# Graph attention with residual layer norm on one core: inverse sums spread from repeated columns, divides between turns, and some transfers issued by ScalarE

## The chip, the cores and the metric

The kernel runs on one core of one Trainium2 chip. The metric is the time of one execution on the device in microseconds (us). The core's engines run side by side and are called TensorE (PE: matmuls, with its weight loads as PEld), VectorE (DVE), ScalarE (ACT), GpSimd (POOL) and SyncE (SP, which here only issues transfers). Sixteen DMA engines move the data.

## What is computed

```python
x (8, 1024, 384) f32, adj (8, 1024, 1024) bool, four 384x384 weights, four biases
q, k, v = heads(x @ Wq + bq), heads(x @ Wk + bk), heads(x @ Wv + bv)      # 6 heads of 64
scores = einsum('bhqd,bhkd->bhqk', q, k) / sqrt(64)
probs = softmax(scores + where(adj, 0.0, -9e15), axis=-1)
ctx = einsum('bhqk,bhkd->bhqd', probs, v)
out = layernorm(x + ctx @ Wf + bf)                                        # eps 1e-5, no affine part
```

## The kernel before

Each of the 8 batches is a list of 24 slots. A slot handles one pair of heads and one tile of 128 queries: TensorE makes the scores of both heads against 1024 keys (`scores`), VectorE adds the mask and takes the row minimum (`mask_scores`, line 676, once per head), ScalarE takes the exponential and the row sum (`exponential`, line 606), and VectorE turns every 32x32 block of the result in place (`turn_squares`, line 683, once per head). Two slots are a group: 256 queries of one pair of heads, 12 groups to a batch. I write g5 for group 5; its second slot is slot 11.

When a group's four turns are done, SyncE issues 16 transfers, `move_square` at line 307, each of which takes 32 partitions of `prob` to 32 partitions of `prob_t` (128 KB). That finishes the transpose of the probabilities. `move(b, group, 0)` issues the first eight and `move(b, group, 1)` the last eight; between the two stand, in some slots, a load of the next batch's x (`load_x`, line 358, slots 4, 6, 11 and 12 by `X_LOADS`), a store of finished rows (line 370) or a load of residual rows (line 364). SyncE works through all this in order. `prob` and `prob_t` have two buffers each, so the masks of group g wait until the transfers of g - 2 have landed.

Two and a half to three slots later TensorE multiplies `prob_t` with v (`mix`, line 515, 16 matmuls in full f32). The rows of the softmax are not divided before that. VectorE takes the reciprocals of the row sums (`invert_sums`, line 688), GpSimd writes them on the diagonals of four 128x128 blocks (`make_diagonal`, line 803), and TensorE multiplies a block of ones with these (`spread_inverses`, line 437), which gives the inverse sums of the queries along the free axis in all 64 partitions of a head. ScalarE copies them to `context` (line 581), and `divide` (line 693) multiplies them with the mix. ScalarE and GpSimd then split the context into a high and a low part (lines 613 and 809) for the output projection.

What else TensorE does stands in the table `STEADY`: per slot a list of jobs, run behind the slot's scores in the order written. ("i", g, ..) is the spread of inverse sums of g, ("m", g, ..) its mix, ("p", n, ..) the output projection of tile n, ("q"/"k"/"v", ..) projections, ("x", ..) transposes of the next batch's x. All jobs but m rotate over three PSUM banks. The other engines follow the same table. In a slot with an m job the order on VectorE is: two masks, two turns, divide. The layer norm's inverse root is 12 tiny steps of Newton's method on GpSimd (`find_root`); the last group of rows of the last batch is scaled on VectorE when they are done.

Of the kernel before, what the change touches and what calls it, by code (L numbers as in the profile page):

```python
# [6 lines left out]
F32 = mybir.dt.float32  # L7
# [3 lines left out]
ALU = mybir.AluOpType  # L11
# [54 lines left out]
X_LOADS = {4: (0, 0), 6: (0, 1), 11: (1, 0), 12: (1, 1)}  # L66
# [51 lines left out]
def graph_attention(nc, x, adj, wq, bq, wk, bk, wv, bv, wf, bf, out):  # L118
# [15 lines left out]
    with ExitStack() as ctx:  # L134
# [22 lines left out]
        diag = sb("diag", [P, 4, P], F32)  # L157
# [4 lines left out]
        ones = sb("ones", [P, HS], F32)  # L162
# [31 lines left out]
        ones_done = sem("ones_done")  # L194
# [11 lines left out]
        diag_done = sem("diag_done")  # L206
# [103 lines left out]

        block = ctx.enter_context(nc.Block())
# [4 lines left out]
        def _(sp):  # L316
# [26 lines left out]
            def move(b, group, part):  # L343
                if part == 0:
                    sp.wait_ge(squared, at(b, UNITS, 4 * group + 4))
                    sp.wait_ge(mixed, at(b, GROUPS, group + 1))
                for ahead in (2 * part, 2 * part + 1):
                    for a in range(4):
                        move_square(sp, group, a, (a + ahead) % 4)

            def load_x(b, half, i):
                last_x = ("x", FT - 1, 1 - half, 1)
                if half == 0 and b.mode == "first":
                    sp.wait_ge(job_done, 3)
                else:
                    sp.wait_ge(job_done, done_through(b, last_x, 1 - half))
                row = S + (4 * half + 2 * i) * P
                sp.dma_start(x_in[:, 2 * i:2 * i + 2, :], x_rows[bass.ds(at(b, S, row), GQ), :].rearrange(
                    "(t p) h -> p t h", p=P)).then_inc(x_loaded[i], 16)
# [13 lines left out]
            def body(b):  # L373
                for s in range(SLOTS):
                    if s % 2 == 1:
                        move(b, s // 2, 0)
                    if s in X_LOADS and b.mode != "last":
                        load_x(b, *X_LOADS[s])
# [4 lines left out]
                    if s % 2 == 1:  # L383
                        move(b, s // 2, 1)
# [15 lines left out]
        def _(pe):  # L400
# [489 lines left out]
```

## Time and profile before

| | us |
|---|---|
| median of 3 runs | 1284.17 (1280.67 to 1289.34) |
| the profiled execution's own time | 1280.71 |
| its span, first to last instruction | 1278.9 |
| TensorE busy | 1177.3 (92%) |
| VectorE busy | 1057.7 (83%) |
| ScalarE busy | 737.2 (58%) |
| GpSimd busy | 655.1 (51%) |
| DMA engines busy, mean | 78.9% on the queue SyncE issues to, 250.13 MB |

The page of the profile gives busy times by engine, a picture of the span in 40 slices, the chain of work that ended last, and groups of instructions by line. Questions to the trace give waits, the chain or the timeline of a stretch in order of time, and busy times of a stretch. An engine's busy share says little here by itself: which wait ends last in a stretch decides.

### The profile page before, as it was taken

The page shows a single profiled execution, that of the slowest core. Times are in us where ns is not written, and L with a number is a line of the kernel's source. Part 1 is how long each engine was busy: PE and PEld are TensorE (multiplying, and loading weights), DVE is VectorE, ACT ScalarE, POOL GpSimd, SP SyncE. Part 2 cuts the span into 40 slices and gives each one's busy share as a digit, 9 for nine tenths or more (in the row PEclk, how much of TensorE's full clock was granted, in tenths as well). Part 3 has the DMA queues.
Part 4 walks back from the last instruction along what each step waited for, and adds up shares of the span by engine and source line. Part 5 has one row for each costly group of instructions (what it writes and reads, how often), then busy time and mean ns, then how long its engine had stood idle before and what let it go on. Part 6 is the DMA issues. An engine that isn't in the chain of part 4 may idle for free.

```text
span 1278.9 us, 23768 instructions
## 1 busy us (share of the span) xinstructions
PE 1177.3 (92%) x8406; PEld 867.3 (68%) x8406; DVE 1057.7 (83%) x1619; ACT 737.2 (58%) x1404; POOL 655.1 (51%) x956
## 2 busy tenths in 40 slices
PE   6998999999999899989999899998999999998874
PEld 5866777666776677666776667766677666776642
DVE  5788887988789887889869889698887988789882
ACT  4665665656556575566655565555664656555540
POOL 1335662646536565474545665355762656535533
PEclk9999999999999999999999999999999999999997
DMA  5678877897778877888877978779877897868883
GB/s 163 148 192 234 190 198 192 201 237 175 201 191 215 228 189 195 198 222 201 205 186 188 237 186 211 181 188 248 190 195 186 205 242 176 206 165 204 211 195 96
DMA packets 111607, 251.66 MB, mean 197 GB/s; under 512 B 27904, under 2 KB 62336, under 8 KB 111488
## 3 DMA queue, kind: packets, MB, share of 16 engines
q1 hardware_dynamic: 111488, 250.13, 78.9%
q8 instruction: 67, 1.10, 0.4%
q14 instruction: 52, 0.43, 0.1%
HBM read 36.11 MB, written 12.58 MB: 38 GB/s over the span
## 4 chain that ended last, share of the span: by engine, by line
PE 53%; SPq 16%; DVE 16%; ACT 5%; issue 4%; DMA 3%; POOL 2%; DVEq 0%; POOLq 0%
PE context_ps L515 17%; SPq L307 15%; PE score_ps L500 13%; PE job_ps L406 7%; DVE prob L683 7%; PE job_ps L408 6%; PE job_ps L407 6%; ACT prob L606 5%; DVE prob L676 5%; DMA prob_t<-prob 3%; PE job_ps L437 2%; DVE res L700 1%; DVE stats L707 1%; POOL xt_lo L793 1%; SPq L370 1%
## 5 line engine op out<-in xcount | busy, mean ns | idle before, releaser
L606 ACT ACTIVATE prob<-prob,row_min 128x1024 f32<-128x1024 f32 x384 | 440.9, 1149 | 252.8 <-DVE row_min L676 252.8
L676 DVE CUSTOM_DVE_ANT_0 prob<-score_ps,mask 128x1024 f32<-128x1024 f32 x384 | 454.7, 1221 | 144.8 <-PE score_ps L500 122.7
L683 DVE STREAM_TRANSPOSE prob<-prob 128x1024 f32<-128x1024 f32 x384 | 458.9, 1233 | 31.7 <-ACT prob L606 31.7
L515 PE MATMUL context_ps<-prob_t,v_all 128*64 128x256 f32 x3072 | 359.8, 388 | 40.0 <-DMA prob_t<-prob 39.8
L515 PEld LDWEIGHTS context_ps<-prob_t,v_all 128*64 128x64 f32 x3072 | 236.0, 140 | 151.3 <-issue 58.6
L775 POOL TENSOR_SCALAR mask<-adj_in 128x1024 f32<-128x1024 uint8 x64 | 68.1, 1064 | 169.6 <-DVE row_min L676 156.2
L500 PE MATMUL score_ps<-k_hi,q_hi 64*128 64x512 f32 x768 | 140.7, 444 | 10.5 <-DVE row_min L676 9.7
L809 POOL TENSOR_TENSOR context_lo<-context,context_hi 128x256 fp32r<-128x256 f32 x96 | 70.6, 735 | 142.0 <-ACT context_hi L613 142.0
L406 PE MATMUL job_ps<-xt_hi,weight_hi 128*128 128x256 f32 (+1 forms) x423 | 142.5, 337 | 0.6
L797 POOL TENSOR_TENSOR q_lo<-raw,q_hi 128x256 fp32r<-128x256 f32 x95 | 69.5, 734 | 139.1 <-ACT raw L598 139.1
L407 PE MATMUL job_ps<-xt_lo,weight_hi 128*128 128x256 f32 (+1 forms) x423 | 135.5, 320 | 0.0
L408 PE MATMUL job_ps<-xt_hi,weight_lo 128*128 128x256 f32 (+1 forms) x423 | 135.5, 320 | 0.0
L500 PE MATMUL score_ps<-k_lo,q_hi 64*128 64x512 f32 x768 | 120.6, 391 | 0.0
L500 PE MATMUL score_ps<-k_hi,q_lo 64*128 64x512 f32 x768 | 119.9, 389 | 0.0
L613 ACT ACTIVATE context_hi<-context 128x256 fp32r<-128x256 f32 x96 | 40.0, 417 | 114.5 <-DVE context L693 114.4
L803 POOL TENSOR_TENSOR diag<-ident,inv_sum 128x512 f32<-128x512 f32 x96 | 100.0, 1042 | 8.6 <-PE job_ps L437 4.3
L301 POOL TENSOR_SCALAR res<-res,mean_var,inv_dev 128x384 f32<-128x384 f32 x62 | 101.9, 1650 | 0.0
L406 PEld LDWEIGHTS job_ps<-xt_hi,weight_hi 128*128 128x128 f32 x423 | 79.5, 188 | 32.3 <-issue 25.9
L500 PEld LDWEIGHTS score_ps<-k_hi,q_hi 64*128 64x128 f32 x768 | 57.2, 184 | 64.1 <-issue 39.0
L797 POOL TENSOR_TENSOR k_lo<-raw,k_hi 128x512 fp32r<-128x512 f32 x46 | 58.8, 1288 | 74.5 <-ACT raw L598 74.4
L581 ACT ACTIVATE context<-job_ps 128x256 f32<-128x256 f32 x96 | 37.0, 386 | 95.4 <-PE job_ps L437 75.4
L408 PEld LDWEIGHTS job_ps<-xt_hi,weight_lo 128*128 128x128 f32 x423 | 79.6, 188 | 6.6
(73 smaller groups left out, 1693.1 us busy)
## 6 DMA issues: line engine op xcount, KB each, us to landing
prob_t<-prob SPq DMA_DIRECT2D x1536, 128.0 KB, 2.4
res<-in_x_dram SPq DMA_DIRECT2D x32, 384.0 KB, 4.0
out_dram<-res SPq DMA_DIRECT2D x32, 384.0 KB, 3.0
x_in<-in_x_dram SPq DMA_DIRECT2D x30, 384.0 KB, 4.1
adj_in<-in_adj_dram SPq DMA_DIRECT2D x31, 256.0 KB, 2.9
res<-in_x_dram SPq DMA_DIRECT2D x1, 768.0 KB, 7.0
prob_t<-in_L_gnn_Wk_dram SPq DMA_DIRECT2D x1, 576.0 KB, 4.3
prob_t<-in_L_gnn_Wq_dram SPq DMA_DIRECT2D x1, 576.0 KB, 8.4
```

The source lines that it names most:

```text
L301: engine.tensor_scalar(res[:, n, :], res[:, n, :], mean_var[:, group % 2, tile, 0:1], inv_dev[:, group % 2, tile:tile + 1], ALU.subtract, ...
L307: queue.dma_start(prob_t[32 * c:32 * c + 32, group % 2, a].rearrange("p q h n -> p (q h n)"), prob[32 * a:32 * a + 32, group % 2, c].rearr ...
L406: pe.matmul(dst, left_hi, right_hi, start=(t == 0), stop=False)
L407: pe.matmul(dst, left_hi, right_lo, start=False, stop=False)
L408: last = pe.matmul(dst, left_lo, right_hi, start=False, stop=(t == FT - 1))
L500: last[head] = pe.matmul(score_ps[:, head, keys], q_part[rows, pair, q], k_part[rows, pair, keys], start=(n == 0), stop=(n == 2))
L515: last = pe.matmul(context_ps[64 * head:64 * head + 64, 0:GQ], v_all[:, kt, col:col + HS], keys, start=(kt == 0), stop=(kt == TT - 1))
L606: nc.scalar.activation(probabilities(t), probabilities(t), ACT.Exp, scale=-1.0, bias=row_min[:, ring:ring + 1], accum_out=row_sum[:, s // ...
L676: nc.vector.tensor_tensor_reduce(probabilities(t), in_quarters(score_ps[:, head, :]), in_quarters(mask[:, s % 2, :]), 1.0, HUGE, ALU.add, ...
L683: nc.vector.transpose(probabilities(t), probabilities(t)).then_inc(squared, 1)
L797: nc.gpsimd.tensor_tensor(lo, copy[:, 0:width], hi, ALU.subtract).then_inc(lo_done, 1)
L803: nc.gpsimd.tensor_tensor(diag[:], ident[:].unsqueeze(1).to_broadcast([P, 4, P]), inv_sum[:, group % 2, :].unsqueeze(2).to_broadcast([P, 4 ...
```

## The change

1. `spread_inverses` no longer multiplies ones with a diagonal. For each head and each tile of 128 queries it takes one column of `inv_sum`, repeated 64 times by a stride of zero, as the weights, and the identity as the moving operand: four matmuls of 128 columns where there were two of 256. `make_diagonal`, its tile and its semaphore are gone; TensorE waits for the reciprocals themselves.
2. On VectorE the divides of a slot stand between its two turns.
3. The loads of x's second half (slots 11 and 12 on SyncE) are issued by ScalarE, both behind its eviction of the job ("x", 2, 0, 1) in slot 11.
4. The last eight squares of the last group of the last batch are issued by ScalarE in place of SyncE.
5. The last Newton iteration of the program runs on VectorE. In slot 9 the output projection stands behind the transpose of x.

```diff
-    9: [("q", 0, 2, 0), ("p", 0, 0, 0), ("x", 0, 0, 1)],
+    9: [("q", 0, 2, 0), ("x", 0, 0, 1), ("p", 0, 0, 0)],
-X_LOADS = {4: (0, 0), 6: (0, 1), 11: (1, 0), 12: (1, 1)}
+X_LOADS = {4: (0, 0), 6: (0, 1)}
...
             def spread_inverses(b, job):
-                pe.wait_ge(diag_done, at(b, GROUPS, job[1] + 3))
-                for head in range(2):
-                    last = pe.matmul(job_bank(b.mode, job)[64 * head:64 * head + 64, 0:GQ], ones[:],
-                                     diag[:, 2 * head:2 * head + 2, :], start=True, stop=True)
+                group = job[1]
+                pe.wait_ge(inverted, at(b, GROUPS, group + 1))
+                for qt in range(2):
+                    for head in range(2):
+                        col = 2 * head + qt
+                        last = pe.matmul(job_bank(b.mode, job)[64 * head:64 * head + 64, qt * P:(qt + 1) * P],
+                                         inv_sum[:, group % 2, col:col + 1].to_broadcast([P, HS]), ident[:],
+                                         start=True, stop=True)
                 last.then_inc(job_done, 1)
...
+                    if s == SLOTS:
+                        move(nc.scalar, b, GROUPS - 1, 1)
...
                             evict(b, job)
+                            if job == ("x", FT - 1, 0, 1):
+                                for i in range(2):
+                                    load_x(nc.scalar, b, 1, i)
...
                         turn_squares(b, 2 * s)
-                        turn_squares(b, 2 * s + 1)
                     for job in work:
                         if job[0] == "m":
                             divide(b, job[1])
+                    if s < SLOTS:
+                        turn_squares(b, 2 * s + 1)
...
                     if s == SLOTS + 1:
-                        dve.wait_ge(root_ops, at(b, 4 * ROOT_OPS, 4 * ROOT_OPS))
+                        dve.wait_ge(root_ops, at(b, 4 * ROOT_OPS, 3 * ROOT_OPS))
+                        find_root(nc.vector, b, 3)
                         scale_rows(nc.vector, 3)
```

In a batch in the middle, these are SyncE's issues of slots 9 to 13 before (line 370 stores rows, 307 moves squares, 364 loads residual rows, 358 loads x):

```order
L370 DMA out_dram<-res 128x2x384
L307 DMA prob_t<-prob 32x1024 x8
L364 DMA res<-in_x_dram 128x2x384
L307 DMA prob_t<-prob 32x1024 x8
L358 DMA x_in<-in_x_dram 128x2x384
L307 DMA prob_t<-prob 32x1024 x8
L358 DMA x_in<-in_x_dram 128x2x384
L307 DMA prob_t<-prob 32x1024 x8
L370 DMA out_dram<-res 128x2x384
```

and these now (383, 303 and 377 are the same issues in the changed file):

```order
L383 DMA out_dram<-res 128x2x384
L303 DMA prob_t<-prob 32x1024 x8
L377 DMA res<-in_x_dram 128x2x384
L303 DMA prob_t<-prob 32x1024 x24
L383 DMA out_dram<-res 128x2x384
```

The two loads of x have left the queue: one stood between the two halves of g5's squares, one ahead of g6's. On ScalarE they stand here now, in slot 11 behind the copies of x and ahead of the next slot's copy of inverse sums and exponentials:

```order
L603 ACTIVATE xt_hi<-job_ps 128x2x8x32
L612 ACTIVATE raw<-job_ps 128x512
L314 DMA x_in<-in_x_dram 128x2x384 x2
L597 ACTIVATE context<-job_ps 128x256
L622 ACTIVATE prob,row_sum<-prob,row_min 128x4x256 x2
```

So whatever ScalarE pays for issuing them lies ahead of slot 12's copy and exponentials.

VectorE in a slot with a mix, before:

```order
L676 ISA prob,row_min<-score_ps,mask 128x4x256
L676 ISA row_min 128x1
L683 STREAM_TRANSPOSE prob<-prob 128x4x256 x2
L693 TENSOR_TENSOR context<-context_ps,context 128x256
L676 ISA prob,row_min<-score_ps,mask 128x4x256
```

and now (697, 704 and 715 are these lines in the changed file):

```order
L697 ISA row_min 128x1
L704 STREAM_TRANSPOSE prob<-prob 128x4x256
L715 TENSOR_TENSOR context<-context_ps,context 128x256
L704 STREAM_TRANSPOSE prob<-prob 128x4x256
L697 ISA prob,row_min<-score_ps,mask 128x4x256
```

The divide, with its wait for the mix, now has a turn behind it instead of the next slot's mask.

## Rows read from the trace of the kernel before

**Rows 1.** The page: busy us of each engine, share of span, instructions.
```profile
PE 1177.3 (92%) x8406; PEld 867.3 (68%) x8406; DVE 1057.7 (83%) x1619; ACT 737.2 (58%) x1404; POOL 655.1 (51%) x956
```
**Rows 2.** The page: the chain that ended last, by engine and by line.
```profile
PE 53%; SPq 16%; DVE 16%; ACT 5%; issue 4%; DMA 3%; POOL 2%; DVEq 0%; POOLq 0%
PE context_ps L515 17%; SPq L307 15%; PE score_ps L500 13%; PE job_ps L406 7%; DVE prob L683 7%; PE job_ps L408 6%; PE job_ps L407 6%; ACT prob L606 5%; DVE prob L676 5%; DMA prob_t<-prob 3%; PE job_ps L437 2%; DVE res L700 1%; DVE stats L707 1%; POOL xt_lo L793 1%; SPq L370 1%
```
**Rows 3.** Waits, whole span: who waited for whom, us in total, times, longest.
```profile
PE context_ps L515 <- DMA prob_t<-prob: 39.8, 26, 3.6
...
DVE prob L676 <- DMA prob_t<-prob: 20.5, 16, 3.0
...
PE job_ps L406 <- POOL context_lo L809: 12.5, 9, 1.9
...
PE job_ps L437 <- POOL diag L803: 4.5, 1, 4.5
```
**Rows 4.** Timeline of TensorE, slot 10 of batch 4: start us, us, what.
```profile
701.14 0.65 PE L437 MATMUL job_ps<-diag,ones 128*64 128x256 f32 x4
...
701.72 0.66 PE L416 MATMUL job_ps<-ident,x_in 128*128 128x128 f32 x4
...
702.31 3.67 PE L515 MATMUL context_ps<-prob_t,v_all 128*64 128x256 f32 x32
```
**Rows 5.** Timeline of SyncE's queue, slots 11 and 12 of batch 4.
```profile
712.82 4.96 SPq L307 DMA_DIRECT2D prob_t<-prob  x8
717.83 0.59 SPq L358 DMA_DIRECT2D x_in<-in_x_dram  x1
718.46 5.08 SPq L307 DMA_DIRECT2D prob_t<-prob  x8
723.58 0.58 SPq L358 DMA_DIRECT2D x_in<-in_x_dram  x1
```
**Rows 6.** Chain of batch 4 in order of time, start us, us, what.
```profile
722.94 3.37 DMA prob_t<-prob
...
726.45 5.36 PE context_ps L515 x32
...
786.48 2.28 DMA prob_t<-prob
```
**Rows 7.** Stretches: busy us by engine, granted clock, DMA share, GB/s.
```profile
719.80:721.20 1.40, 1.40 (x14) 1.40 (x13) 1.40 (x3) 0.67 (x2) 1.01 (x3) 1.00 0.95 343
...
721.60:724.40 2.80, 2.25 (x16) 1.27 (x16) 2.63 (x4) 2.80 (x8) 2.80 (x3) 1.00 1.04 250
1250.00:1255.00 5.00, 0.48 (x4) 0.32 (x4) 0.45 (x2) 0.42 (x1) 3.91 (x14) 0.75 0.91 207
```
**Rows 8.** Timeline of ScalarE, end of slot 11 and slot 12 of batch 4.
```profile
712.36 0.60 ACT L596 ACTIVATE raw<-job_ps 128x512 f32<-128x512 f32 x1
713.79 0.38 ACT L581 ACTIVATE context<-job_ps 128x256 f32<-128x256 f32 x1 [0.83 <-PE job_ps L437]
715.79 1.15 ACT L606 ACTIVATE prob<-prob,row_min 128x1024 f32<-128x1024 f32 x1 [1.61 <-DVE row_min L676]
```
**Rows 9.** Chain of the program's end in order of time.
```profile
1247.39 0.51 SPq L307
...
1256.81 2.44 DMA prob_t<-prob
...
1271.37 0.18 DVE var_eps L714
1271.57 0.18 DVE inv_dev L717
...
1275.11 0.48 DVE res L301
```
**Rows 10.** Timeline of VectorE, slot 12 of the last batch.
```profile
1175.92 1.23 DVE L676 CUSTOM_DVE_ANT_0 prob<-score_ps,mask 128x1024 f32<-128x1024 f32 x1 [0.27 <-DMA prob_t<-prob]
...
1181.23 1.23 DVE L676 CUSTOM_DVE_ANT_0 prob<-score_ps,mask 128x1024 f32<-128x1024 f32 x1
```

More of the change, by code:

```diff
@@ L309, in move_square, with load_x, find_root, result @@
                             ).then_inc(landed[group % 2], 16)
+        def load_x(queue, b, half, i):
+            last_x = ("x", FT - 1, 1 - half, 1)
+            if half == 0 and b.mode == "first":
+                queue.wait_ge(job_done, 3)
+            else:
+                queue.wait_ge(job_done, done_through(b, last_x, 1 - half))
+            row = S + (4 * half + 2 * i) * P
+            queue.dma_start(x_in[:, 2 * i:2 * i + 2, :], x_rows[bass.ds(at(b, S, row), GQ), :].rearrange(
+                "(t p) h -> p t h", p=P)).then_inc(x_loaded[i], 16)
+        def find_root(engine, b, group):
+            engine.wait_ge(guess_done, at(b, 4, group + 1))
+            guess, var = inv_dev[:, group % 2], var_eps[:, group % 2]
+            ops = 0
+            def result(instruction):
+                nonlocal ops
+                ops += 1
+                instruction.then_inc(root_ops, 1)
+                engine.wait_ge(root_ops, at(b, 4 * ROOT_OPS, group * ROOT_OPS + ops))
+            for _ in range(NEWTON_STEPS):
+                result(engine.tensor_tensor(newton[:], guess, guess, ALU.mult))
+                result(engine.tensor_tensor(newton[:], newton[:], var, ALU.mult))
+                result(engine.tensor_scalar(newton[:], newton[:], -0.5, 1.5, ALU.mult, ALU.add))
+                result(engine.tensor_tensor(guess, guess, newton[:], ALU.mult))
+        def move(queue, b, group, part):
+            queue.wait_ge(squared, at(b, UNITS, 4 * group + 4))
+            queue.wait_ge(mixed, at(b, GROUPS, group + 1))
+            for ahead in (2 * part, 2 * part + 1):
+                for a in range(4):
+                    move_square(queue, group, a, (a + ahead) % 4)
         block = ctx.enter_context(nc.Block())
@@ L341, in load_adjacency @@
                     "(q p) k -> p q k", p=P)).then_inc(adj_loaded, 16)
[L343 to L359, printed above, removed]
             def load_residual(b, group):
@@ L382, in body @@
                         load_residual(b, RES_LOADS[s])
-                    if s % 2 == 1:
-                        move(b, s // 2, 1)
+                    if s % 2 == 1 and (s < SLOTS - 1 or b.mode != "last"):
+                        move(sp, b, s // 2, 1)
                     if s % 6 == 1 and (s // 6 < 3 or b.mode != "last"):
@@ L840, in body @@
                         next_mask(b, s // 6 + 1, s % 6 - 4)
-                    if s == 2 and b.mode == "first":
-                        make_diagonal(b, 0)
-                    for job in work:
-                        if job[0] == "m" and job[1] + 1 < GROUPS:
-                            make_diagonal(b, job[1] + 1)
                     for group in contexts_split(b.mode, s):
```

39 lines of the change are left out of this document (5 added, 34 removed).

## The prediction

> **What bounds the kernel now.** I read the page first. TensorE is busy 92% of the span and VectorE 83% [rows 1], but the chain that ended last is TensorE for only 53%; SyncE's queue holds 16% and VectorE 16% [rows 2]. So the bound changes inside a batch. The chain in order of time shows where: from the end of a batch to about slot 6 it is an unbroken row of matmuls, and from slot 7 on it passes VectorE, SyncE's issues, a landing and the mix. The waits say the same in sum: TensorE waits 39.8 us for landed squares in 26 places and VectorE another 20.5 us in 16 [rows 3]. Out of 1279 us that is not much, so a change that removes no TensorE work can give only a few per cent at most. The queue's timeline shows the tightest place, slots 11 and 12: eight squares, a load of x, eight squares, a load of x, without a pause [rows 5]. The last square of g5 is issued at 722.94, takes 3.37 us to land, and the mix waits for it until 726.45; a square with no load around it lands in 2.28 us [rows 6].
>
> **The change part by part.** All sums are against the profiled execution's own 1280.71 us; the median of the runs, 1284.17, is 3.5 us above it, and I shift by that at the end.
>
> *The spread.* Before, one spread holds TensorE from 701.14 to 701.72, 0.58 us, for four records of 256 columns (each f32 matmul leaves two) [rows 4]. They run in two pairs, one for each 64-wide half of the array. Now there are eight records of 128 columns, four pairs. No row has 64-wide weights with 128 columns. The nearest is the transpose of x: four records of 128 columns, each with its own 128x128 f32 weights, hold TensorE from 701.72 to 702.31, 0.59 us [rows 4]. So a new weight load per 128 columns does not lengthen the record, and four pairs should take what four such records take. The mix behind it (32 records, 64-wide weights, in 3.67 us) shows that pairs do overlap. I take +0.02 us a spread. If pairs did not overlap, eight records would cost twice the 0.59, so the other bound is +0.6 us; below, zero, since the columns streamed are the same. There are 96 spreads, and the chain has 2% of the span in L437 [rows 2], 25.6 us, or 44 spreads at 0.58. The rest lie ahead of a mix that waits for its landing anyway. Sum: 44 x 0.02 = +1 us (0 to +26).
>
> *The diagonal gone.* GpSimd loses 96 operations, but TensorE waited for one only once, 4.5 us [rows 3], ahead of the last mix, which waits longer for its landing. The context's low part no longer stands behind a diagonal, and the divide comes a turn earlier, so TensorE's wait for it, 12.5 us in 9 places [rows 3], should vanish, helped by x standing ahead of the projection in slot 9. I count almost nothing: where I looked at it, in slot 9, the chain runs through VectorE's turns, which have no gap there. That cover gone, it would be worth 1.3 us a batch. I take -0.5 us for all of it.
>
> *The divide between the turns.* VectorE does the same work. The price comes where the mix is not done when the first turn ends, since the second turn then waits too, and the next mask behind it. In slot 12 of the last batch mask and mix start together at 1175.9, released by the same landing. The mix needs 3.67 us [rows 4]; the next mask ran at 1181.23, behind both turns and the divide [rows 10]. With the new order the divide starts at 1179.6, when the mix ends, and the turn ends about 1.6 us later, at 1181.2. The next mask is where it was, within 0.1 us, and it needs the scores, which TensorE only starts behind the mix. So the cost is zero as long as the divide waits for nothing else; uncovered it would be 0.1 us in the 11 even slots of 8 batches, +9 us. I take 0.
>
> *The loads of x.* Per batch but the last, SyncE's queue loses two issues of 0.59 and 0.58 us [rows 5]. The first stands inside g5's chain, so its last square is issued 0.63 us earlier. It also has company in landing now (3.37 against 2.28 us), and that need not get better: both loads are issued by ScalarE from 712.96 on, where the copy of x ends, all inside g5's transfers. ScalarE can afford it: it has 0.83 us of idle time before the next copy, which would slip by about 0.4 us, and 1.61 us before the next exponential [rows 8]. The DMA engines are what is short. With squares alone and a backlog they moved 250 GB/s at a share of 1.04, against 207 GB/s at 0.91 when one queue feeds them at its own pace [rows 7]. In the microsecond and a half in which mostly a load ran, the rate was 343 GB/s [rows 7]. Work from 712.8 on: 16 squares, 2.1 MB at 250 GB/s, 8.4 us; two loads and the residual rows issued just before, 1.18 MB at 343 GB/s, 3.4 us; with about a microsecond for the first packet and the landing that ends at 725.6, where it was 726.3. Where the queue was late for g6 as well, more is won. I take -0.9 us a batch: 7 x 0.9 = -6.3 us. Bounds: the second load's 0.39 MB at the squares' 250 GB/s, 1.6 us, less the issue of 0.63, is a loss of 1.0 us each, +7 us; and the issue with all of the late landing, 0.6 + 1.1 us, plus the 0.6 us where g6 finds the queue still busy, is -2.3 us each, -16 us.
>
> *The last squares.* The chain has 16 issues from 1247.39 on, the last at 1256.81, and the landing at 1259.25 [rows 9]. Split over two queues, if only issuing counts, the last is issued 8 x 0.63 = 5.0 us earlier. If the DMA engines count, 2.10 MB at 250 GB/s take 8.4 us from about 1248.1 and land at 1256.9: -2.3 us. At 207 GB/s nothing is won. I take -2.3 (0 to -5.0), for both halves read the same 32 partitions of `prob` in the same order.
>
> The Trainium skill has a rule here, in "SBUF — State Buffer", Door 1: The DMA port swizzle: 32 neighbouring partitions reach only 8 of 16 DMA ports, about 218 GB/s at most. By it, since both queues would start from the same 32 partitions, the 2.10 MB would take 9.6 us and the saving would be 1.1 us. The 207 GB/s agree with it, the 250 GB/s do not, so it holds at most for squares that share their partitions.
>
> *Newton on VectorE.* Its last tiny step starts at 1271.57, 0.20 us behind the one before it, and the scaling at 1275.11, 3.54 us later, with 12 steps of GpSimd between [rows 9]. Thirteen steps of 0.20 are 2.6 us: -0.9 us (0 to -1).
>
> Sum: +1 - 0.5 + 0 - 6.3 - 2.3 - 0.9 = **-9.0 us**, to 1271.7 in the profile and **1275 us** in the median, 0.7% less.
>
> **The rivals.** *The queue's relief pays in full (0.22).* TensorE's clock speaks for it. Before g5's mix it idled and then ran the mix in 5.36 us instead of 3.67 [rows 4, 6]. If the earlier landing saves that too, each batch gives up to -2.3, and the end 5.0: 1 - 0.5 - 16 - 5.0 - 0.9 = -21, 1263 us. Against it: the DMA engines are already saturated in this stretch [rows 7].
>
> *The transfers only trade places (0.20).* The engines, not the queues, set g5's landing and the end's. Then the loads give 0 and the end, by the port rule or by 207 GB/s, 1 us or none: 1 - 0.5 - 1 - 0.9, about -1, 1283 us. For it speaks the share of 1.04 [rows 7].
>
> *The short matmuls don't overlap (0.10).* It is the one that ends slower: 44 spreads at +0.6 are +26 us, less the other gains of 10, +16: 1300 us. It decides against the change from +0.23 us a spread on. Against it stands the transpose's 0.59 us for as many weight loads at twice the width [rows 4].
>
> **How the numbers follow.** The forecast has 0.48, and by itself 1268 to 1282. The likeliest value is 1275. The range takes in most of the first rival and all of the second, and cuts off the last: 1263 to 1289. This kernel's runs spread over 0.7%, so about 1% is what a measurement can tell from no change; that is below 1271.3 or above 1297. Faster: the first rival and the forecast's lower edge, 0.29. Slower: the last rival where nothing else pays, 0.08. Same: 0.63.
>
> **What would show it.** The mix should start 0.6 us behind a spread, as now; 1.0 or more means that pairs don't overlap. g5's last landing should come 12.6 us behind its first issue instead of 13.5, and ScalarE's two issues should cost it no idle exponential. The last group's squares should land 9.5 us after their first issue, not 11.9. TensorE's wait for the context's low part should be near nothing, and the scaling should start 2.6 us behind the guess. It would be wrong if VectorE's new wait for the mix grew to over 0.3 us a slot, or if SyncE's issues took longer than 0.59 us while ScalarE issues too.

## The result, and the profile after

| | before | after |
|---|---|---|
| median, us | 1286.29 (4 runs) | 1306.65 (1296.31 to 1312.39, 4 runs) |
| ratio | | 1.0149 [1.0109, 1.0189] |
| profiled execution, us | 1280.71 | 1307.82 |
| its span, us | 1278.9 | 1305.9 |
| mean granted clock of TensorE | 0.986 | 0.972 |

The change makes the kernel 1.5% slower. I had forecast 1275 us, 0.7% less, and the time lies outside the range.

The page of after, busy time by engine and the chain that ended last, beside [rows 1, 2]:

```profile
PE 1191.2 (91%) x8790; PEld 889.9 (68%) x8790; DVE 1062.6 (81%) x1631; ACT 735.6 (56%) x1404; POOL 555.6 (43%) x847
...
PE 53%; SPq 14%; DVE 13%; DMA 5%; ACT 5%; issue 5%; POOL 3%; ACTq 1%; POOLq 0%; DVEq 0%
```

TensorE is busy 14 us more with the same arithmetic, GpSimd 100 us less without the diagonals, and the chain now has 5% in landings where it had 3%. The waits of after, beside [rows 3] (who waited for whom, us in total, times, longest):

```profile
PE context_ps L532 <- DMA prob_t<-prob: 69.1, 26, 8.0
...
DVE context L715 <- PE context_ps L532: 43.9, 43, 13.8
...
DVE prob L697 <- DMA prob_t<-prob: 36.0, 21, 5.1
```

TensorE waits for landed squares in 26 places as before, but 69.1 us where it was 39.8; VectorE's masks wait 36.0 instead of 20.5, and the divide now waits for the mix.

Where in a batch? I worked out from both traces, as means over batches 1 to 6, when each group's squares landed and what the mixes did:

| mean over batches 1 to 6, us | before | after |
|---|---|---|
| length of a batch | 153.7 | 158.2 |
| g4: last issue's end to last landing | 1.71 | 5.00 |
| g5: the same | 2.55 | 3.78 |
| g6: the same | 1.94 | 1.71 |
| idle of TensorE before the mixes of g4, g5, g6 | 0.59, 2.49, 0.13 | 4.01, 0.14, 2.80 |
| first start to last start in those mixes | 3.29, 4.39, 3.27 | 5.06, 3.25, 4.84 |

(A mix at full clock measures 3.24 to 3.30 here; the timeline adds the last record's own length.) Batch 0 is 148.1 and 148.3 us, and the last batch 182.4 in both, to the end of the program. So the whole loss of the profiled execution, 27 us of span, is 6 x 4.4 us in the middle batches. (By the medians the change costs 20 us: the profiled execution of before is the fastest of its four.) It lies in three slots: g4's squares, which had landed in time, are late, and the mixes of g4 and g6 run long.

Batch 4 shows why. SyncE's queue in after, beside [rows 5] (start us, us, what):

```profile
725.13 4.96 SPq L303 DMA_DIRECT2D prob_t<-prob  x8
730.13 0.58 SPq L377 DMA_DIRECT2D res<-in_x_dram  x1
730.81 20.34 SPq L303 DMA_DIRECT2D prob_t<-prob  x24
```

The first line is the last eight squares of g4, issued until 730.09; then the residual rows, then g5's sixteen squares and eight of g6, without the loads of x between. ScalarE in after, beside [rows 8]:

```profile
728.22 1.15 ACT L622 ACTIVATE prob<-prob,row_min 128x1024 f32<-128x1024 f32 x1
729.07 0.41 ACTq L314 DMA_DIRECT2D x_in<-in_x_dram  x1
...
729.51 0.76 ACTq L314 DMA_DIRECT2D x_in<-in_x_dram  x1
...
730.56 0.60 ACT L612 ACTIVATE raw<-job_ps 128x512 f32<-128x512 f32 x1
732.00 0.38 ACT L597 ACTIVATE context<-job_ps 128x256 f32<-128x256 f32 x1 [0.84 <-PE job_ps L453]
```

The loads stand in the program behind the copy of x, L612. They leave at 729.07 and 729.51, the first while ScalarE is still in an exponential, and the copy ends only at 731.16. The queue of ScalarE hands over the first DMA while five operations that stand ahead of it, the copy the last, have yet to start; nothing made it wait. So the loads go out 2.1 us before the copy's end, the first 1.02 us before g4's last issue ends. The chain of the stretch, beside [rows 6], shows what that does:

```profile
729.50 4.60 DMA prob_t<-prob
734.10 0.14 issue
734.23 0.93 PE context_ps L532 x5
```

The last square of g4 takes 4.60 us to land, where a square with no load around it took 2.28 and g5's last one, with a load in its own queue, 3.37 [rows 6]. The packets show who is served in the meantime. From 730.75 to 732.00 (queue: packets, MB, share of the 16 engines):

```profile
q10 hardware_dynamic: 151, 0.23, 75.5%
q1 hardware_dynamic: 15, 0.00, 0.7%
```

q10 is ScalarE's queue, q1 SyncE's. g4's last square has been issued and has not landed, and for 1.25 us all the bytes that move are those of the loads. TensorE's timeline of the same batch:

```profile
731.29 0.66 PE L453 MATMUL job_ps<-ident,inv_sum 128*64 128x128 f32 x8 [0.68 <-DVE res L722]
734.23 5.36 PE L532 MATMUL context_ps<-prob_t,v_all 128*64 128x256 f32 x32 [2.28 <-DMA prob_t<-prob]
...
745.25 0.66 PE L453 MATMUL job_ps<-ident,inv_sum 128*64 128x128 f32 x8
...
760.26 6.26 PE L532 MATMUL context_ps<-prob_t,v_all 128*64 128x256 f32 x32 [4.26 <-DMA prob_t<-prob]
```

and stretches of it (us, busy us by engine with counts, then the granted clock, DMA share, GB/s):

```profile
734.30:736.00 1.70, 1.70 (x12) 1.26 (x14) 1.70 (x3) 0.52 (x1) 1.21 (x7) 0.66 1.12 346
736.00:739.50 3.50, 3.50 (x24) 2.32 (x20) 1.84 (x3) 1.87 (x4) 0.72 (x4) 0.68 1.03 247
745.80:749.40 3.60, 3.60 (x36) 2.21 (x34) 3.44 (x7) 2.84 (x6) 3.27 (x4) 1.00 0.55 121
```

Having idled for 2.28 us, TensorE runs g4's mix in 5.36 us; the granted clock is 0.66 and 0.68 of full, that is, 1.2 GHz for about two thirds of it. g5's mix, at 745.73 behind matmuls without a gap, has 1.00, 2.4 GHz, and takes 3.6 us. g6's is late again: 4.26 us idle, then 6.26 us. Before the change the same fall was paid once in four of the batches 1 to 6, at g5; after it twice in five of them, at g4 and g6.

The end of the program, SyncE's and ScalarE's queues and the chain, beside [rows 9]:

```profile
1275.76 7.26 SPq L303 DMA_DIRECT2D prob_t<-prob  x8
```

```profile
1275.76 7.93 ACTq L303 DMA_DIRECT2D prob_t<-prob  x8
```

```profile
1299.47 0.18 DVE inv_dev L739
...
1302.12 0.48 DVE res L297
```

Each queue takes over 7 us for eight issues, where one alone took 5. The last landing came at 1286.57, 10.81 us behind the first issue; it was 11.86 before. The scaling starts 2.65 us behind the guess.

### The profile page after: what moved, and what is told of

Read it like the earlier page. It is cut to its first block, busy times and chain, and to the rows that moved or that the text cites. A ratio compares the mean times of both kernels' runs of the same rounds, so it can differ in the third digit from the quotient of the medians.

```text
span 1305.9 us, 24453 instructions
## 1 busy us (share of the span) xinstructions
PE 1191.2 (91%) x8790; PEld 889.9 (68%) x8790; DVE 1062.6 (81%) x1631; ACT 735.6 (56%) x1404; POOL 555.6 (43%) x847
## 4 chain that ended last, share of the span: by engine, by line
PE 53%; SPq 14%; DVE 13%; DMA 5%; ACT 5%; issue 5%; POOL 3%; ACTq 1%; POOLq 0%; DVEq 0%
PE context_ps L532 19%; SPq L303 13%; PE score_ps L517 13%; PE job_ps L419 7%; PE job_ps L421 6%; PE job_ps L420 6%; DVE prob L704 6%; DMA prob_t<-prob 5%; ACT prob L622 5%; DVE prob L697 4%; PE job_ps L453 2%; POOL xt_lo L816 1%; SPq L383 1%; DVE res L722 1%; DVE stats L729 1%
## 5 line engine op out<-in xcount | busy, mean ns | idle before, releaser
L704 DVE STREAM_TRANSPOSE prob<-prob 128x1024 f32<-128x1024 f32 x384 | 467.0, 1236 | 31.7 <-ACT prob L622 31.7
L532 PE MATMUL context_ps<-prob_t,v_all 128*64 128x256 f32 x3072 | 375.0, 400 | 69.1 <-DMA prob_t<-prob 69.1
L532 PEld LDWEIGHTS context_ps<-prob_t,v_all 128*64 128x64 f32 x3072 | 239.3, 144 | 175.8 <-issue 88.0
L798 POOL TENSOR_SCALAR mask<-adj_in 128x1024 f32<-128x1024 uint8 x64 | 67.1, 1048 | 180.5 <-DVE row_min L697 167.3
L517 PEld LDWEIGHTS score_ps<-k_lo,q_hi 64*128 64x128 f32 x768 | 72.6, 184 | 16.7
L517 PEld LDWEIGHTS score_ps<-k_hi,q_lo 64*128 64x128 f32 x768 | 72.7, 184 | 16.4
```

The lines of the kernel that those rows point to most:

```text
L517: last[head] = pe.matmul(score_ps[:, head, keys], q_part[rows, pair, q], k_part[rows, pair, keys], start=(n == 0), stop=(n == 2))
L532: last = pe.matmul(context_ps[64 * head:64 * head + 64, 0:GQ], v_all[:, kt, col:col + HS], keys, start=(kt == 0), stop=(kt == TT - 1))
L704: nc.vector.transpose(probabilities(t), probabilities(t)).then_inc(squared, 1)
```

## The experiments

Ratios are to the kernel before, with 95% intervals. Line numbers in a diff are left out.

**Parts undone and parts alone.** First, which part costs: after without the moved loads, and before with the loads, the spread or the divide alone. e1:

```diff
-X_LOADS = {4: (0, 0), 6: (0, 1)}
+X_LOADS = {4: (0, 0), 6: (0, 1), 11: (1, 0), 12: (1, 1)}
-                            if job == ("x", FT - 1, 0, 1):
-                                for i in range(2):
-                                    load_x(nc.scalar, b, 1, i)
```

> The changed kernel with part 3 undone: SyncE issues both loads of x's second half again, in slots 11 and 12; all other parts stay. Theory Q (ScalarE's queue issues the loads ahead of its copies, while g4's last squares are still to land, and they overtake these): g4 lands 1.7 us behind its last issue again instead of 5.0, slots 11 and 12 shrink from 17.2 to about 12.2 us a batch, and the time is 1280 us or less, ratio to before 0.99 to 1.00. Rival V (the divide between the turns, or the spread, costs the time): nothing of this changes, the time stays near 1306, ratio 1.015.

Measured: 1.0002 [0.997, 1.0035], 1288.97 us. The whole loss is gone. Theory Q had hoped for more, 1280 us or less; slots 11 and 12 take 12.8 us in the trace, and g4's lag is 1.71.

e2 is before with the same lines the other way round:

```diff
-X_LOADS = {4: (0, 0), 6: (0, 1), 11: (1, 0), 12: (1, 1)}
+X_LOADS = {4: (0, 0), 6: (0, 1)}
+                            if job == ("x", FT - 1, 0, 1):
+                                for i in range(2):
+                                    load_x(nc.scalar, b, 1, i)
```

> The kernel before with part 3 alone: ScalarE issues both loads behind the job (x, 2, 0, 1) of slot 11. Theory Q: g4 lands 4 to 5 us behind its last issue, 3 to 5 us more a batch, ratio 1.015 to 1.025. Rival V: ratio 0.995 to 1.002.

Measured: 1.0095 [1.0062, 1.0129], 1303.37 us. The loads alone cost 1%, less than the 1.5 to 2.5% of theory Q and far more than rival V allows; g4's lag is 4.47 us. The profiled execution took 1289.82 us, the fastest of its ten, so what I read from the trace of e2 below is on the low side.

e3 is before with the new spread and inversion, and without diagonals:

```diff
-                    last = pe.matmul(job_bank(b.mode, job)[64 * head:64 * head + 64, 0:GQ], ones[:],
-                                     diag[:, 2 * head:2 * head + 2, :], start=True, stop=True)
+                        last = pe.matmul(job_bank(b.mode, job)[64 * head:64 * head + 64, qt * P:(qt + 1) * P],
+                                         inv_sum[:, group % 2, col:col + 1].to_broadcast([P, HS]), ident[:],
+                                         start=True, stop=True)
```

> The kernel before with part 1 alone: inverse sums spread from repeated columns, no diagonals on GpSimd. Theory Q: the spread costs TensorE 0.02 us more each, GpSimd is free 100 us more, ratio 0.998 to 1.001. Rival V: if repeated columns or the earlier waits cost anything, ratio above 1.003.

Measured: 0.9993 [0.9966, 1.002], 1286.42 us. e4 is before with the divide between the turns:

```diff
-                        turn_squares(b, 2 * s + 1)
                     for job in work:
                         if job[0] == "m":
                             divide(b, job[1])
+                    if s < SLOTS:
+                        turn_squares(b, 2 * s + 1)
```

> The kernel before with part 2 alone: the divide between a slot's two turns. Theory Q: VectorE waits for the mix in the middle of some slots, but its next mask needs scores that come behind the same mix, so ratio 0.998 to 1.002. Rival V: the wait delays turns and masks, 0.1 us or more in each of the 11 even slots with a mix and up to 1.5 us where the mix runs at 1.2 GHz, ratio 1.005 to 1.015.

Measured: 0.9999 [0.9968, 1.0029], 1288.49 us. Spread and divide, alone, are worth nothing either way, within 0.3%. Loads alone (1.0095) do not make up all of after's 1.0149, and the divide is a candidate for the rest. I took after again beside the next kernels, unchanged, and e7, which is e2 with the diff of e4:

> The changed kernel as it is, again, so that the next three stand on the same chip beside it. Ratio to before 1.012 to 1.018.

> The kernel before with parts 2 and 3, the divide between the turns and the loads on ScalarE. If the two add up to nothing more than part 3 alone, its ratio is that of the loads alone, 1.0095. If the divide's wait for a late mix makes the late landing dearer, it is 1.013 to 1.018, as the whole change.

```diff
 # e2, and:
-                        turn_squares(b, 2 * s + 1)
                     for job in work:
                         if job[0] == "m":
                             divide(b, job[1])
+                    if s < SLOTS:
+                        turn_squares(b, 2 * s + 1)
```

Measured: after again 1.0135 [1.0089, 1.0181]; e7 1.0198 [1.0164, 1.0232], 1314.55 us. So a divide that costs nothing alone doubles the price of the loads. e7 came out dearer than I had expected, and dearer than after, which has the same two parts and more; between the profiled executions 6 of the 7 us lie in batch 0, where g4's squares land 4.80 us behind their last issue in e7 and 1.87 us in after. The waits of e7:

```profile
PE context_ps L515 <- DMA prob_t<-prob: 62.3, 23, 4.8
...
DVE context L696 <- PE context_ps L515: 51.2, 47, 10.2
```

and the one of e2:

```profile
PE context_ps L515 <- DMA prob_t<-prob: 51.6, 25, 4.5
```

In these two traces TensorE waits 11 us longer for about as many landings.

**Where the loads leave, and in which queue.** Three kernels keep all of after and change only this. e5 gives both loads back to SyncE, directly ahead of g5's squares, so that they cannot pass g4's:

```diff
                 for s in range(SLOTS):
+                    if s == 11 and b.mode != "last":
+                        for i in range(2):
+                            load_x(sp, b, 1, i)
                     if s % 2 == 1:
                         move(sp, b, s // 2, 0)
```

(ScalarE's two loads behind its copy of x are taken out here, and in e6 as well.)

> The changed kernel with both loads of x issued by SyncE in slot 11, back to back, directly ahead of g5's squares: the same bytes within about 1.5 us of the time at which ScalarE issued them, but in the queue of the squares and behind g4's. If it is the second queue that lets the loads overtake g4's squares, g4 lands 1.7 to 1.9 us behind its last issue (5.0 in the changed kernel), and the ratio to before is 0.998 to 1.005, the two issues now being paid in full ahead of g5. If it is simply 0.79 MB of loads in a saturated stretch, g4 is still late by 2 us or g5 by 3 us or more, ratio 1.008 or more.

Measured: 1.0042 [1.0014, 1.0069], 1295.29 us. e6 lets ScalarE issue them behind slot 12's exponentials, where by its queue they fall among g5's squares alone, which is where my prediction had put them:

```diff
                         exponential(b, 2 * s + 1)
+                    if s == 12 and b.mode != "last":
+                        for i in range(2):
+                            load_x(nc.scalar, b, 1, i)
```

> The changed kernel with ScalarE's two loads behind the exponentials of slot 12. Their masks wait for g4's landing, so the loads can't be issued before it, and everything they meet is g5's squares, as the prediction had it. If the prediction's size for that was right, g4 lands 1.7 us behind its last issue, g5's landing gains 0.9 us a batch, and the ratio to before is 0.990 to 0.996. If loads on a second queue hold up any squares they meet, g5 lands 4 to 5 us behind its last issue instead of 2.5, ratio 1.005 or more.

Measured: 1.009 [1.0068, 1.0113], 1301.97 us. e9 leaves them in their place but makes ScalarE's queue wait until its copy of x is really done:

```diff
                             if job == ("x", FT - 1, 0, 1):
+                                act.wait_ge(job_out, out_through(b, job))
                                 for i in range(2):
                                     load_x(nc.scalar, b, 1, i)
```

> The changed kernel with a wait of ScalarE for its own copy of x ahead of the two loads, so that they are issued where the prediction had them, behind the copy, about 2 us later than in the changed kernel. If the sequencer's running ahead of its queued activations is what put the loads among g4's squares, no square of g4 is issued behind the first load now, g4 lands 1.7 to 2.5 us behind its last issue, g5 lands 3.5 to 4.7 us behind its last, and the ratio is 1.003 to 1.010, as with the loads behind slot 12's exponentials. If the place made no difference, g4 stays at 5 us and the ratio at 1.0135.

Measured: 1.0106 [1.0074, 1.0138], 1299.27 us. Means over batches 1 to 6, worked out from the traces:

| us | before | after | e5 | e6 | e9 |
|---|---|---|---|---|---|
| g4: last issue's end to landing | 1.71 | 5.00 | 1.70 | 1.70 | 1.81 |
| g5: last issue's end to landing | 2.55 | 3.78 | 2.81 | 4.70 | 4.95 |
| g5: first issue to last landing | 13.63 | 14.11 | 13.59 | 15.40 | 15.48 |

In e6 and e9 the first load leaves at most 0.33 us before g4's last issue ends, mostly after it, and g4 lands as before the change. So the overtaking made it late: its lateness goes when the loads leave later, with the same bytes in the same second queue. But the lateness then falls on g5, whose squares take 15.4 us instead of 13.6. In one queue, e5, g5's squares have nearly their old lag, but the first is issued 1.9 us behind the last turn instead of 0.7, and g5's mix is waited for 3.48 us and is slow in five of the six batches. e6's timeline of TensorE shows the two mixes side by side:

```profile
725.50 3.67 PE L532 MATMUL context_ps<-prob_t,v_all 128*64 128x256 f32 x32
...
739.43 6.58 PE L532 MATMUL context_ps<-prob_t,v_all 128*64 128x256 f32 x32 [3.30 <-DMA prob_t<-prob]
```

and its stretches, same columns as above:

```profile
725.50:729.00 3.50, 3.50 (x34) 2.60 (x32) 3.27 (x8) 1.81 (x4) 2.84 (x9) 1.00 0.95 258
739.50:743.50 4.00, 4.00 (x20) 2.54 (x22) 3.55 (x5) 2.38 (x4) 0.00 (x0) 0.50 0.95 242
```

g4's mix follows without a gap at 2.4 GHz, g5's comes behind 3.30 us of idling and starts at exactly half. The DMA engines move 242 to 258 GB/s at a share of 0.95 in both: I take them to be full, so that a load can only be fitted in by making squares wait.

**The clock as the channel.** A late landing is paid twice, as idle time and then as a slow mix. I sorted the batches 1 to 6 of ten traces (before, after, its repeat, e1 to e7) by how many mixes took over 4.2 us:

| slow mixes in the batch | batches | mean length, us | range | idle before its 12 mixes, mean us |
|---|---|---|---|---|
| 0 | 15 | 153.1 | 152.1 to 154.0 | 4.3 |
| 1 | 30 | 155.3 | 153.6 to 157.6 | 4.4 |
| 2 | 15 | 159.0 | 157.7 to 160.9 | 7.4 |

The groups hardly overlap, whatever the kernel. Over its whole trace before has 6 slow mixes, after 13, e1 4, e2 7, e7 16. Between none and one the idle time is the same, and the batch is 2.2 us longer: that is what one slow mix goes with. The second slow mix comes together with 3 us more of idling, so there the table does not say which of them costs. To part them I kept the waits and filled the idle time with matmuls nobody reads, five in e10 ahead of the mixes of g4 and g6. Their result is overwritten by the mix:

```diff
                 pe.wait_ge(context_done, at(b, GROUPS, group + 2))
+                if group in (4, 6) and b.mode != "last":
+                    for _ in range(5):
+                        pe.matmul(context_ps[:, GQ:2 * GQ], ident[:], v_all[:, 0, 0:GQ],
+                                  start=True, stop=True)
```

> The changed kernel with five idle matmuls (identity by 256 columns of v, into the unused half of the mix's PSUM bank, read by nobody) in front of the mixes of g4 and g6 in all batches but the last, where TensorE now waits 4.0 and 2.8 us for landed squares. They leave the late landing as it is and keep TensorE at work. Theory C (the late landing costs what it costs because TensorE falls to 1.2 GHz in those waits, and then runs the mix in 5.0 instead of 3.3 us with everything behind it): granted clock 0.98 or more instead of 0.97, mixes of g4 and g6 at 3.3 us, batches of 153 to 155 us instead of 158, ratio to before 0.998 to 1.005. Theory L (the lateness itself costs it): batches stay at 157 to 158 us, or grow by the idle work, ratio 1.012 to 1.02.

Measured: 1.0083 [1.0055, 1.0111], 1296.68 us, granted clock 0.986, 4 slow mixes. The ratio lies between the two theories. The mixes of g4 and g6 fall from 5.06 and 4.84 to 3.58 and 3.30 us, and a batch from 158.2 to 155.5. Batch 0, where g4 had not been late, is 151.1 us instead of 148.3 with the fill; the last batch, without a fill, is 182.4 us as in after. So of the 4.4 us a batch that the change lost in these traces, 2.7 went by the clock; by the ratios of all runs it is 0.7 of 1.5%, or nearly half. The rest stays with late landings.

e11 puts the same fill, four matmuls, in e1 ahead of g5's mix, e12 in before, and e15 is e11 again:

```diff
+                if group in (5, 99) and b.mode != "last":
+                    for _ in range(4):
+                        pe.matmul(context_ps[:, GQ:2 * GQ], ident[:], v_all[:, 0, 0:GQ],
+                                  start=True, stop=True)
```

> The changed kernel with both loads back on SyncE, as in e1_loads_back, and four idle matmuls (1.7 us) in front of the mix of g5, where it waits about 2.2 us. Theory C: no batch but the last has a mix at 1.2 GHz, all batches take 152.5 to 153.5 us, ratio to before 0.990 to 0.997. Theory L: ratio 1.000 to 1.005.

> The kernel before with four idle matmuls in front of the mix of g5 in all batches but the last, and nothing else. Theory C: the gain of e11_back_filled is the clock's, so this has it too, ratio 0.991 to 0.996, no mix of batches 0 to 6 at 1.2 GHz. If that gain needs the changed parts (spread, divide, Newton, tail), the ratio is 0.997 to 1.002.

> e11_back_filled again, on the chip of the one before: what the parts of the change other than the loads add once the clock holds. Theory C, with the prediction's sizes for them (-2.7 us): 0.2% below e12_before_filled. If the divide between the turns costs something of its own, 0 to 0.3% above it.

Measured: e11 0.9914 [0.9887, 0.994], 1276.39 us; e12 0.9917 [0.989, 0.9943], 1278.23 us; e15 0.9893 [0.9856, 0.993], 1275.25 us. The fill makes either kernel about 1% faster. e15 is 3 us below e12 in the median, as the prediction's sizes for the other parts have it (-2.7 us), but the intervals overlap. e11 in batch 4:

```profile
724.60 1.99 PE L526 MATMUL context_ps<-v_all,ident 128*128 128x256 f32 x8
...
726.97 3.67 PE L535 MATMUL context_ps<-prob_t,v_all 128*64 128x256 f32 x32 [0.38 <-DMA prob_t<-prob]
```

```profile
727.00:730.50 3.50, 3.50 (x32) 2.18 (x32) 3.27 (x5) 2.17 (x3) 0.82 (x1) 1.00 0.95 250
```

The fill ends 0.38 us before the squares have landed, and the mix has the full clock, where before the change it took 5.36 us [rows 6]. In the traces the mixes of g5 fall from a mean of 4.39 us in before to 3.30 in both e11 and e12. Yet the traces show less than the whole of the gain: the middle batches are 153.7 us in before, 153.5 in e12, 153.0 in e11 and 152.9 in e1. The reason is which execution was profiled. Those of before and e1 are each the fastest of their own runs, and e1's had the g5 mixes of batches 1 to 6 at full clock without a fill. The 93 runs of before that were taken beside the experiments have granted clocks of 0.971 to 0.987; the 15 below 0.977 took 1293.3 us on average, the 12 from 0.984 on 1283.0, and a straight line through all gives 9.3 us for 0.01. The six runs of e12 have 0.990 on average where before has 0.980: by that line, an estimate, 9 us, and 9.7 were measured between the medians. The last batch, in which nothing is filled, adds something in one kernel: it is 182.4 and 183.3 us in before and e1, 180.5 in e12, but 177.1 in e11 and 177.8 in its repeat e15, with fewer or other slow mixes. The runs may also scatter less: over ten runs each, by 8.8 us in e11 and by 13.0 in e1. So that the fill helps is measured, and that it does so by the clock agrees with the clocks of all runs; why the last batch is shorter in e11 and e15 stays open. e11 is the best kernel of this study: parts 1, 2, 4 and 5 with the fill. Its interval and e12's lie on each other, so its gain is the fill's.

One thing more can be read from these numbers, and it limits what e10 said. e10 and e11 differ only in who issues the loads and in which gaps are filled and how far, and they ran side by side: 1296.68 against 1276.39 us, 1.6%. Without fills, after and e1 are 1.5% apart. e13 below against e12 is 1.2%, without fills e2 against before 1.0%. So with fills on both sides, moving the loads costs as much as it did. Only a part of that is still the clock: it is 0.984 in e10 and 0.990 in e11 over all runs, some 6 of the 20 us by the line above. The clock explains part of what after lost against a before that itself loses it at g5; the late landings are a price of the move that these fills do not take away.

e13 and e14 use the fill of e10 to ask why the divide made the loads dearer: e13 is e2 with it, e14 is e7 with it.

```diff
+                if group in (4, 6) and b.mode != "last":
+                    for _ in range(5):
+                        pe.matmul(context_ps[:, GQ:2 * GQ], ident[:], v_all[:, 0, 0:GQ],
+                                  start=True, stop=True)
```

> The kernel before with the loads on ScalarE (as e2_loads_only, 1.0095) and five idle matmuls in front of the mixes of g4 and g6. Theory C: few slow mixes, what is left is the lateness and the idle work, ratio 1.002 to 1.007.

> The same with the divide between the turns (without the idle matmuls, e7_loads_divide, 1.0198). If the divide makes the loads dearer only through the clock, the idle matmuls take away nearly all of the difference: within 0.3% of e13_loads_filled, ratio 1.004 to 1.009. If VectorE's wait in mid-slot costs by itself, the difference of 1% stays: 1.012 to 1.018.

| | unfilled | filled |
|---|---|---|
| loads alone (e2, e13) | 1.0095 [1.0062, 1.0129] | 1.0033 [1.0008, 1.0057] |
| loads and divide (e7, e14) | 1.0198 [1.0164, 1.0232] | 1.0026 [1.0002, 1.0051] |

e14's ratio is lower still than I had expected, 1.004 at least. With the idle time filled the two can't be told apart: the medians are 1291.58 and 1293.85 us, 0.2% apart, where the ratios without fill differ by 1.0%. So the divide raises the loads' price through the clock, wholly or nearly so; the two intervals would hide a remainder of some 0.3%. How it does so I can argue but did not show: slot 10 is 5.19 instead of 5.53 us with it, the loads leave 1.7 us before g4's last issue ends instead of 1.3 on average, more squares stand behind them, and TensorE idles longer and loses the clock in 16 mixes instead of 7 (in the traces; over all runs the granted clock is 0.965 against 0.976). After's own batches fit: in batch 0 no square was issued behind the first load and g4's lag was 1.87 us, with one square it was 4.0 and 4.2, with two 4.9, with three 5.2, with four 5.7 and 6.1. The time seems to matter more than the count: in three batches of e2 no issue of a square began behind the first load, but it left 0.54 to 0.86 us before g4's last issue ended, and the lag was 3.9 to 4.1.

**The last squares.** e8 is e1 with ScalarE's eight squares started from the other half of the partitions, since the port rule that the prediction named would have made the shared partitions the limit:

```diff
             for ahead in (2 * part, 2 * part + 1):
-                for a in range(4):
+                for n in range(4):
+                    a = (n + 2) % 4 if queue is nc.scalar else n
                     move_square(queue, group, a, (a + ahead) % 4)
```

> The changed kernel with the loads back on SyncE, and of the last group's squares ScalarE's eight in another order, so that the two queues never read the same 64 partitions at a time (sources 2, 3, 0, 1 against 0, 1, 2, 3). In the changed kernel the sixteen landed 10.8 us behind the first issue, 11.9 before. If the ports of the source partitions are the limit, as the page on SBUF has it for 32 partitions, it is 8.5 us or less now; if the limit is elsewhere (issuing, or the engines' own rate of about 250 GB/s), it stays at 10 to 11 us. The time of the whole is 1.000 in ratio, within what can be measured.

Measured: 0.997 [0.9941, 1.0], 1285.03 us. The last landing is 10.91 us behind the first issue, against 10.69 in e1 and 10.81 in after. Reading from other partitions gains nothing here. But the edit moves more than the sources. A square goes from block a to block (a + ahead) % 4: in after both queues read the same 32 partitions and write to opposite halves, in e8 they read from opposite halves and write the same blocks in the same order, 0, 1, 2, 3, 1, 2, 3, 0. So e8 takes the sharing away on the reading side and puts it on the writing side. It shows that shared sources alone are not the limit; it does not show that ports are none. It did change the issues: eight take 6.4 us in either queue, not 7.2 to 7.9 as in e1 and after, and then the last landing comes 4.5 us behind them, not 2.9 to 3.2.

## Why the prediction was wrong

**The loads of x: the failed step.** The prediction had both loads "issued by ScalarE from 712.96 on, where the copy of x ends, all inside g5's transfers", and took -0.9 us a batch, -6.3 in all. The move cost the whole 1.5% instead: with it undone (e1) the ratio is 1.0002. Two things in it were wrong. The place: ScalarE's queue issued them 2.1 us before the copy ended, up to 2.7 us before g4's last issue ended, so that they also hit a group that I had counted as safe. I read the order of the program as the order of time; this DMA, without a wait, went when the queue reached it. The Trainium skill has the ground for that in "Advanced Engine Details and Errata", Sequencer and Instruction Queues: engine instructions are pushed into a queue (8 deep on ScalarE by its table), where they wait, and others can be read meanwhile. It doesn't speak of a DMA there. The trace agrees, with five operations not yet started ahead of the first load. The size: with the place as predicted, e6 and e9, g5's landing came 15.4 and 15.5 us behind its first issue, where I had 12.6 and before had 13.6. I had credited the queue with 0.6 us and said that the DMA engines were full at a share of 1.04, but then spread the loads' cost evenly over bytes. What counts is who is served first. In one queue a load behind the squares came behind them; from a second queue it was served among them. "DMA: Bandwidth & Descriptors", Queues, rings and completion order, of the Trainium skill, says that an engine takes turns between queues, packet by packet. That both are served at a time agrees with the trace, where g4's lag goes from 1.71 to 5.00 us; even turns it does not show, since for 1.25 us of batch 4 the loads had all the bytes. My bound of +7 us for this step was the second load's bytes less the issue, 1.0 us a batch; the landing of g5 alone moved by 1.8 in e6.

**The clock: on one side only.** I knew that TensorE idles before g5's mix and then runs it in 5.36 us, and used that for the rival that ends faster. No rival had a landing that gets later and so costs the clock at a second mix. That is what happened: 2.7 of the 4.4 us a batch in the traces, nearly half by all runs. My only slower rival, matmuls that don't overlap, was looked for in the wrong part.

**The queue's relief** never reached g5: its squares landed 14.11 us behind their first issue, 13.63 before. That its mix is waited for only 0.14 us instead of 2.49 is no gain, since everything stands later by then, behind g4's.

**The spread: right.** Eight records take 0.66 us where four took 0.65; I had taken +0.02. e3 is 0.9993.

**The diagonal gone: right in kind.** TensorE never waits for it, and its wait for the context's low part fell from 12.5 us in 9 places to this, in after:

```profile
PE job_ps L419 <- POOL context_lo L824: 2.6, 3, 1.9
```

It gave nothing that e3 could measure.

**The divide: right alone**, 0.9999, and wrong beside the loads. The condition I had put down, that "the divide waits for nothing else", does not hold once g4's and g6's mixes are late: VectorE idles 1.72 and 1.48 us before their divides. With the fills even that costs nothing that shows.

**The last squares: direction right, size off.** 10.81 us instead of 11.86, -1.05 us, where I took -2.3. That pair flatters it: the ten traces with two queues have 10.69 to 11.90 us, 11.2 on average, the eight with one queue 11.74 to 12.54, 12.0 on average, so about -0.8. My sum had a slip as well: 8.4 us from 1248.1 end at 1256.5, not 1256.9. "If only issuing counts" failed as a bound, since two queues that issue side by side take 7.3 and 7.9 us for eight issues instead of 5.0. The port rule of the Trainium skill ("SBUF — State Buffer", Door 1: The DMA port swizzle), for shared source partitions, gave nearly the right figure, 1.1 us, as an estimate. e8 does not bear it out: with other sources the time is the same. But e8 made the destinations shared, so ports on the writing side stay untested. That two queues slow each other's issues is seen; what sets the 10.8 us I leave open.

**Newton on VectorE: right**, 2.65 us instead of 3.54.

## What to carry to other kernels

Moving a DMA to a second queue does not only relieve the first: it takes away the protection that the first queue's order gave to the transfers somebody waits for, and ScalarE's queue issued it as early as its waits allowed, not where it stood among ScalarE's work. e9's wait for the copy moved it there. Where the DMA engines are full, leave what is not urgent behind what is urgent, in the same queue. Where TensorE must wait for data by a few microseconds before a long run of matmuls, look at the granted clock behind the wait, and try a few unread matmuls in the gap before you rearrange transfers: here four of them a batch went with 0.8 to 1.1%, more than I had forecast for all five parts of the change. It is no cure for a late landing: with the gaps filled, the moved loads still cost 1.2 to 1.6%.

## What I had not expected of the hardware

- ScalarE's queue issued a DMA while five earlier operations of ScalarE had not started, 2.1 us before the end of the last of them.
- What a second queue's 0.79 MB costs the first depends on who is ahead by a hair: g4's lag was 1.84 to 1.87 us where the first load left 0.29 to 0.36 us before g4's last issue ended (batch 0 of after, its repeat and e2), 3.9 and 4.0 us at 0.54 and 0.57 us (e2), 6.1 at 2.5 us.
- Issues slow each other: eight by one queue alone take 5.0 us, eight by each of two queues 7.3 and 7.9.
- At f32, eight 64-wide matmuls of 128 columns, their weights one column repeated by a stride of zero, take 0.66 us, four of 256 columns with ordinary weights 0.65.
- With unread matmuls at g5 of the earlier batches, the last batch, which has none, came out 5 to 6 us shorter in e11 and e15, 2 us in e12; with those at g4 and g6 (e10) it stayed as it was.
- Behind 2.3 to 4.3 us of idling the granted clock was 0.50 to 0.68 over most of a mix, and 1.00 with 0.38 us. Not every wait did it: before's g5 mix in batch 5 followed 3.30 us of idling and took 3.67 us, full clock. Over the twelve traces without fills, 1 of 938 mixes was slow behind less than 1 us of idling, 17 of 37 behind 2.0 to 2.5, 12 of 17 behind 3.0 to 3.5, and all 32 behind more than 4. What decides in between I leave open.
